# Local attention after a convolution block on one core: score tiles of 96 near keys, P turned in 32x32 blocks, values after the fourth unit

## What is computed

```python
perceived = conv3x3_depthwise(x, w_perc) + b_perc           # 128 -> 384 channels
hid = gelu(perceived @ w_up1 + b_up1)                       # 256 channels
h = x + hid @ w_up2 + b_up2
q, k, v = split(h @ w_qkv + b_qkv)
scores = stack([(q * shift(k, dy, dx)).sum(-1) for dy, dx in _POS]) / sqrt(128)   # 9 neighbours
out = h + sum_i softmax(scores)[i] * shift(v, dy_i, dx_i)
```

## Time and profile before

| | |
|---|---|
| median of 3 runs | 483.28 us (482.9 to 489.4) |
| profiled execution | 483.21 us, span of its instructions 481.4 us |
| PE busy | 443.8 us (92%), 2964 matmuls |
| DVE busy | 367.3 us (76%) |
| ACT busy | 230.4 us (48%) |
| POOL busy | 197.2 us (41%) |
| convolution matmuls (line 359) | 1728 of 256 columns, 285 to 327 ns in the record |
| scores (line 401) | 256 instructions of 192 columns, 326 ns |
| masks (line 397) | 64 of 384 columns, 329 ns |
| transposes (line 417) | 128 of 128 columns, 273 ns |
| values (line 431) | 320 of 32 to 192 columns, 305 ns |
| exponential (line 590) | 128 of 197 columns, 423 ns |
| GpSimd normalisation (line 919) | 31 of 768 elements, 1468 ns |

### The profile page before, as it was taken

The page is one execution under the profiler, slowest core; times in us unless marked ns, Lnnn a source line. Parts: engine busy times, 40 slices in busy tenths (PEclk is TensorE's granted clock), DMA queues, the critical chain, the costliest instruction groups (busy, mean ns, idle before and its releaser), DMA issues.

```text
span 481.4 us, 8443 instructions
## 1 busy us (share of the span) xinstructions
PE 443.8 (92%) x2964; PEld 388.9 (81%) x2964; DVE 367.3 (76%) x728; ACT 230.4 (48%) x491; POOL 197.2 (41%) x154
## 2 busy tenths in 40 slices
PE   1448899999999999999999999999999999999994
PEld 1437789797979899797979899797979899797863
DVE  5998768878695968878695968778695968765644
ACT  2443264554627454553627454553627354552633
POOL 3555636354451525354451525354452525320201
PEclk9966999999999999999999999999999999999999
DMA  8101020403103040403103040403013020301011
GB/s 283 70 0 60 0 103 0 146 2 100 47 21 126 2 146 0 145 0 105 40 17 128 0 145 0 145 0 113 32 26 119 0 87 0 89 9 38 0 46 44
DMA packets 11509, 29.31 MB, mean 61 GB/s; under 512 B 2400, under 2 KB 3168, under 8 KB 11488
## 3 DMA queue, kind: packets, MB, share of 16 engines
q1 hardware_dynamic: 10784, 29.03, 17.8%
q10 hardware_dynamic: 704, 0.02, 0.1%
HBM read 20.65 MB, written 8.39 MB: 60 GB/s over the span
## 4 chain that ended last, share of the span: by engine, by line
PE 81%; issue 4%; ACT 2%; DVE 1%; POOLq 0%; POOL 0%; ACTq 0%; DVEq 0%
PE m_ps L359 38%; PE work L372 11%; PE work L431 9%; PE s_ps L401 8%; PE work L378 5%; PE work L383 5%; PE work L417 3%; PE s_ps L397 2%; ACT hid L545 0%; ACT thi L529 0%; ACT p_sb L590 0%; DVE y L738 0%; POOLq L84 0%; POOL p_sb L919 0%; ACT L590 0%
## 5 line engine op out<-in xcount | busy, mean ns | idle before, releaser
L359 PE MATMUL m_ps<-thi,whi 128*128 128x256 f32 x576 | 188.6, 327 | 15.0 <-POOL wlo L928 7.1
L359 PE MATMUL m_ps<-tlo,whi 128*128 128x256 f32 x576 | 164.1, 285 | 0.0
L359 PE MATMUL m_ps<-thi,wlo 128*128 128x256 f32 x576 | 164.1, 285 | 0.0
L359 PEld LDWEIGHTS m_ps<-thi,whi 128*128 128x128 f32 x576 | 111.2, 193 | 23.3 <-issue 14.9
L919 POOL TENSOR_TENSOR p_sb<-p_sb,rsum 128x768 f32<-128x768 f32 x31 | 45.5, 1468 | 176.3 <-DVE rsum L780 176.3
L359 PEld LDWEIGHTS m_ps<-tlo,whi 128*128 128x128 f32 x576 | 111.6, 194 | 7.2 <-issue 7.2
L359 PEld LDWEIGHTS m_ps<-thi,wlo 128*128 128x128 f32 x576 | 111.2, 193 | 0.0
L912 POOL TENSOR_TENSOR tlo<-t,thi 128x1088 fp32r<-128x1088 f32 (+1 forms) x32 | 64.2, 2027 | 44.4 <-ACT thi L529 44.4
L590 ACT ACTIVATE p_sb<-s_ps,negmax 128x197 f32<-128x197 f32 x124 | 51.4, 423 | 37.6 <-DVE negmax L773 37.6
L607 ACT ACTIVATE q_sb<-work,bq_s 128x512 f32<-128x512 f32 x32 | 22.0, 689 | 85.2 <-PE work L378 85.1
L372 PE MATMUL work<-hid,w2T 128*128 128x512 f32 x120 | 54.1, 593 | 1.5 <-ACT hid L545 1.5
(11 more groups left out here) (110 smaller groups left out, 663.9 us busy)
## 6 DMA issues: line engine op xcount, KB each, us to landing
xp<-x_planes SPq DMA_DIRECT2D x16, 680.0 KB, 5.2
xr<-x_rows SPq DMA_DIRECT2D x16, 512.0 KB, 4.0
out<-o_sb SPq DMA_DIRECT2D x32, 256.0 KB, 4.1
w1T<-w SPq DMA_DIRECT2D x1, 384.0 KB, 3.3
mask_bf<-masks SPq DMA_DIRECT2D x1, 192.0 KB, 3.9
w2T<-w SPq DMA_DIRECT2D x1, 128.0 KB, 4.9
wqk_in<-w_qk SPq DMA_DIRECT2D x1, 128.0 KB, 4.8
ident<-identity SPq DMA_DIRECT2D x1, 64.0 KB, 4.8
```

The lines of the kernel that those rows point to most:

```text
L359: last = pe.matmul(m_ps[:, b, col:col + S], a[:, j, dy, half * P:(half + 1) * P], c[:, par, T_PLACE[j], dy * WIN:dy * WIN + S], start=(s = ...
```

## The change

**Scores.** A tile's query row now meets only its own three key rows: 96 key columns (`NEAR`) instead of 192. For each of the four image rows of a tile there is one product of 32 queries and 96 keys whose result lies in partitions 32 x row onwards, so it uses a strip of 32 columns of the array. Four tiles share one bank at a step of 128 columns; `scores(n, g)` is one mask product of 4 x 96 columns and 16 such products, and both groups stand after unit 6. In `p_sb` column block dk of a row of queries holds the key row dk - 1 away. The maximum is one reduction for four tiles, the exponential has 101 columns, the normalisation 384 elements.

**Turning P.** The transposes on TensorE, their copies and `edges` are gone. `turn_p(n, g)` on VectorE turns four tiles' P in 32x32 blocks, 128 partitions x 384, into `ptc`. Since each block must go to the partitions of its key row, `place_p(n)` on ScalarE copies twelve sets of blocks (4 rows of queries x 3 key rows, 32 partitions x 8 tiles x 32, two of them 7 tiles) from `ptc` to `pt`.

**Order.** `values(n, 0)` and `values(n, 1)` stand together after unit 3 and wait for all twelve copies. On VectorE `combine(n, 1)` goes ahead of the first turn and of the second reciprocal, the second turn goes between `combine_y(n, 1)` and `finish_y(n, 1)`, and from body 2 on `combine(n, 0)` goes ahead of `add_h(n, 0)`. The fp32 identity and its load are gone.

```diff
-KEYS = WINDOW + NZ
-STEP = 256
+NEAR = 3 * W
+KEYS = NEAR + NZ
+STEP = P
...
+        ptc = sb("ptc", [P, T, NEAR])
...
+        def s_bank(g):
+
+            return s_ps[:, g, :].rearrange("p (t k) -> p t k", k=STEP)
...
+            def scores(n, g):
+                if from_image(n, 2):
+
+                    pe.wait_ge(p_done, n * 8 + (4 * g - 12))
+                s = s_bank(g)[:, :, 0:NEAR]
+                pe.matmul(s, ident_bf[:, :], mask_bf[:, g:g + 4, :], start=True, stop=False, skip_group_check=True)
+                for u in range(4):
+                    for row in range(TR):
+                        q = ((4 * g + u) * TR + row) * W
+                        last = pe.matmul(s[row * W:(row + 1) * W, u, :], q_sb[:, q:q + W], h_around[:, q:q + NEAR],
+                                         start=False, stop=(u == 3 and row == TR - 1), skip_group_check=True)
                 last.then_inc(s_ready, 1)
...
             def values(n, g):
 
 
                 pe.wait_ge(v_done, n * 4 - 4)
-                pe.wait_ge(pt_done, n * 2 + (g - 3))
-                pe.wait_ge(edges_done, n * 4 + (2 * g - 6))
+                pe.wait_ge(z_done, n * 4 - 4)
+                pe.wait_ge(pt_done, n * PLACED - PLACED)
...
                 units(0)
-                if store:
-                    transpose_p(n - 1, 1)
-                units(1)
+                units(1, 2, 3)
                 if store:
                     values(n, 0)
-                units(2)
-                if store:
                     values(n, 1)
-                units(3)
...
                     project_v(n, 3)
-                    scores(n, 2)
-                units(8)
-                if attn:
-                    scores(n, 3)
-                units(9, 10, 11)
-                if attn:
-                    transpose_p(n, 0)
+                units(8, 9, 10, 11)
...
+            def place_p(n):
+
+                if isinstance(n, int) and n == 1:
+                    act.wait_ge(zeroed, 3)
+                act.wait_ge(ptc_done, n * 2)
+                if from_image(n, 2):
+                    act.wait_ge(o_ready, n * 2 - 2)
+                for row in range(TR):
+                    for dk in range(3):
+                        shift, near = divmod(row + dk - 1, TR)
+                        first, end = max(0, -shift), min(T, T - shift)
+                        col = (near + 2 - dk) * W
+                        nc.scalar.copy(pt[near * W:(near + 1) * W, first + shift:end + shift, col:col + W],
+                                       ptc[row * W:(row + 1) * W, first:end, dk * W:(dk + 1) * W]).then_inc(pt_done, 1)
...
                 if attn:
-                    take_pt(n, 0)
-                if is_last(n):
-                    take_pt(n, 1)
+                    place_p(n)
...
+            def row_max(n, g):
+
+                s = s_bank(g)
+                dve.wait_ge(s_ready, n * 2 + (g - 1))
+                for j in (2 * g, 2 * g + 1):
+                    z = v_bank(n, j)[:, 0:2 * VT].rearrange("p (t c) -> p t c", c=VT)[:, :, C:VT]
+                    dve.wait_ge(v_ready, n * 4 + (j - 3))
+                    nc.vector.tensor_tensor(s[:, 2 * j - 4 * g:2 * j - 4 * g + 2, NEAR:KEYS],
+                                            z.to_broadcast([P, 2, NZ]), z_base[:, 2 * j:2 * j + 2, :],
+                                            ALU.add).then_inc(z_done, 1)
+                dve.wait_ge(z_done, n * 4 + (2 * g - 2))
+                nc.vector.tensor_reduce(negmax[:, 4 * g:4 * g + 4], s[:, :, 0:KEYS], AX.X, ALU.max,
                                         negate=True).then_inc(rmax_done, 1)
...
+            def turn_p(n, g):
 
                 if is_last(n) and g == 1:
                     dve.wait_ge(pn_last_done, 1)
                 else:
                     dve.wait_ge(pn_done, n * 2 + (g - 1))
...
+                if from_image(n, 2):
+                    dve.wait_ge(pt_done, n * PLACED - PLACED)
+                tiles = slice(4 * g, 4 * g + 4)
+                nc.vector.transpose(ptc[:, tiles, :], p_sb[:, tiles, 0:NEAR]).then_inc(ptc_done, 1)
...
                 if more:
                     transform_ab(n + 1, 1 - par)
+                if from_image(n, 2) and conv:
+                    combine(n, 0)
                 if store:
                     add_h(n, 0)
...
-                if from_image(n, 2):
-                    if conv:
-                        combine(n, 0)
-                    if attn:
-                        sum_h(n, par)
+                if from_image(n, 2) and attn:
+                    sum_h(n, par)
...
-                if attn:
-                    sums(n, 1)
-                    edges(n, 0)
                 if conv:
                     combine(n, 1)
+                if attn:
+                    turn_p(n, 0)
+                    sums(n, 1)
+                if conv:
                     combine_y(n, 1)
+                if attn:
+                    turn_p(n, 1)
                 if conv:
                     finish_y(n, 1)
-                if attn:
-                    edges(n, 1)
```

More of the change, by code:

```diff
@@ L54, in window_masks @@
 def window_masks(dtype):
-    m = np.full((P, 4, WINDOW), NEG, dtype)
-    for kind in range(4):
+    m = np.full((P, T // 2 + 1, NEAR), NEG, dtype)
+    for kind in range(T // 2 + 1):
         for qy in range(TR):
             for qx in range(W):
-                for ky in range(-1, TR + 1):
-                    if abs(ky - qy) > 1 or (kind == 0 and ky < 0) or (kind == 3 and ky >= TR):
+                for dk in range(3):
+                    if (kind == 0 and qy + dk == 0) or (kind == T // 2 and qy + dk == TR + 1):
                         continue
                     for kx in range(max(0, qx - 1), min(W, qx + 2)):
-                        m[qy * W + place(qx), kind, (ky + 1) * W + place(kx)] = 0.0
+                        m[qy * W + place(qx), kind, dk * W + place(kx)] = 0.0
     return m
@@ L211, in build @@
         rsum_done = sem("rsum_done")
-        edges_done = sem("edges_done")
+        ptc_done = sem("ptc_done")
+        pt_done = sem("pt_done")
         pn_last_done = sem("pn_last_done")
@@ L222, in build @@
         N_W = 8
+        PLACED = TR * 3
         def steady(eng, body, last=None):
@@ L385, in project_v @@
                 last.then_inc(v_ready, 1)
-            def scores(n, j):
-                if is_last(n) and j >= 2:
-                    if j == 3:
-                        pe.wait_ge(z_done, n * 4 - 2)
-                elif j >= 2 or from_image(n, 2):
-                    pe.wait_ge(p_done, n * 8 + (2 * j - 10))
-                s = s_bank(n, j).rearrange("p (a b) -> p a b", a=2)
-                kinds = 0 if j == 0 else 2 if j == T // 2 - 1 else 1
-                pe.matmul(s[:, :, 0:WINDOW], ident_bf[:, :], mask_bf[:, kinds:kinds + 2, :], start=True, stop=False,
-                          skip_group_check=True)
-                for u in range(2):
-                    i = 2 * j + u
-                    last = pe.matmul(s[:, u, 0:WINDOW], q_sb[:, i * P:(i + 1) * P],
-                                     h_around[:, i * P:i * P + WINDOW], start=False, stop=(u == 1),
-                                     skip_group_check=True)
-                last.then_inc(s_ready, 1)
@@ L406, in transpose_p @@
-            def transpose_p(n, g):
-                if is_last(n) and g == 1:
-                    pe.wait_ge(pn_last_done, 1)
-                else:
-                    pe.wait_ge(pn_done, n * 2 + (g - 1))
-                if is_last(n):
-                    pe.wait_ge(z_done, n * 4 - 3 if g == 0 else n * 4)
-                else:
-                    pe.wait_ge(z_done, n * 4 + (0 if g == 0 else -2))
-                for u in range(4):
-                    last = pe.transpose(work[:, 1 + g, u * P:(u + 1) * P], p_sb[:, 4 * g + u, W:W + P], ident[:, :])
-                last.then_inc(pt_ready, 1)
+            def scores(n, g):
[8 more added lines that the diff above has]
+                                         start=False, stop=(u == 3 and row == TR - 1), skip_group_check=True)
+                last.then_inc(s_ready, 1)
@@ L787, in edges @@
                     dve.wait_ge(pn_done, n * 2 + (g - 1))
-                first, end = 4 * g, 4 * g + 4
-                a = max(first, 1)
-                nc.vector.transpose(pt[P - W:P, a - 1:end - 1, P + W:WINDOW],
-                                    p_sb[0:W, a:end, 0:W]).then_inc(edges_done, 1)
-                e = min(end, T - 1)
-                nc.vector.transpose(pt[0:W, first + 1:e + 1, 0:W],
-                                    p_sb[P - W:P, first:e, P + W:WINDOW]).then_inc(edges_done, 1)
+                if from_image(n, 2):
+                    dve.wait_ge(pt_done, n * PLACED - PLACED)
+                tiles = slice(4 * g, 4 * g + 4)
+                nc.vector.transpose(ptc[:, tiles, :], p_sb[:, tiles, 0:NEAR]).then_inc(ptc_done, 1)
             def add_h(n, g):
@@ L918, in normalise @@
                 pool.wait_ge(rsum_done, n * 2 + (g - 1))
```

(5 more changed lines are left out.)

69 lines of the change are left out of this document (19 added, 50 removed).

## The result

The changed kernel takes 567.49 us (median of 4 runs, 566.5 to 571.52) against 483.61 us for the kernel before (4 runs), a ratio of 1.172 with a 95% interval of 1.161 to 1.183: slower by 84 us. I had forecast 548 us, range 515 to 580. The profiled execution has a span of 565.6 us; that of before has 481.4.

What follows compares the result with a forecast made beforehand. TensorE was taken to bound the kernel at 27.0 us an image. Standstill 50, clock 10, last body 3.5, end 2.4, less 1.2 at the start, make 65 us on 483.2: 548 us, range 515 to 580.

Steps and rivals of the forecast that it cites:

- P late: Ahead of the values: the second turn stands behind combine_y, then twelve copies follow; P ready at +7.95, TensorE at +4.25.
- the standstill behind unit 3: TensorE ahead of the first value matmul, bodies 2 to 15: stands still for 3.7 us waiting for ScalarE's copies.
- the chain behind the copies: Gelu, m13, combine, add_h, transform and add_h(1) queue behind the copies; up(1) ends at +15.2, an image takes 30.6 us.
- the fallen clock: TensorE's granted clock falls after the standstill in most images, adding 0.7 us an image.
- E + 4.15: On VectorE: end of the second turn, counted from E, the moment unit 0 of the next image begins.
- the copy: ScalarE's copies of P to pt: 0.31 us each, twelve take 3.8 us; bounds 2.3 and 4.8 us.
- S: The new score stage on TensorE, masks and small products: 3.5 us an image, ends 1.8 and 5.7.
- Strips fully side by side: Rival, score stage: all four strips overlap, S = 1.8, 27 us less, 521 us; chance 15%.
- Strips in a row: Rival, score stage: products follow one another, S = 5.7, 35 us more, 583 us; chance 15%.
- the clock holds: Rival, TensorE: the clock does not fall, 10 us less, 538 us; chance 20%.
- combine_y escapes GpSimd: Rival, VectorE: the copies start 2.05 us earlier, 29 us less, 519 us; chance 8%.
- P is in time: Rival, values: copies end by +4.25, TensorE alone sets the time, 474 us, or 446 us with side-by-side strips; chance 7%.

Runs made afterwards that it cites:

- Half of the copies: Changed kernel with only six of the twelve sets of blocks copied to pt, part of P left out: 519.6 us, ratio to before 1.070.
- the early turns: Changed kernel with, on VectorE, the second reciprocal ahead of combine(n, 1) and both turns directly behind it, ahead of combine_y: 510.83 us, ratio to before 1.051.
- the split copies: The early turns plus add_h ahead of combine(n, 0), with VectorE copying four sets and ScalarE the other eight: 471.83 us, ratio to before 0.976.
- the filler: Changed kernel with 36 convolution-sized matmuls, results unread, put between unit 3 and the values: 549.84 us, ratio to before 1.133.
- The run with the other order: Changed kernel with the loops of the twelve copies swapped, key row outside and query row inside: 568.25 us, ratio to before 1.168.
- the run with four products in one strip: Changed kernel with the score loops over tile and row swapped, so four products in a row use the same 32-column strip: 596.33 us, ratio to before 1.229.
- the two versions in which P is in time: The split copies, 471.83 us; and the same with VectorE taking five sets, ScalarE seven, and add_h(1) ahead of the transform, 459.92 us.

## Why the prediction was right, and where its terms were off

**Direction and mechanism: right.** P late, the standstill behind unit 3, the chain behind the copies, the fallen clock: each was seen where it was put. Half of the copies (-48 us) and the early turns (-57 us) show that the lateness of P is the cause, the split copies on top of these take the whole loss away, and the filler shows the clock's own share. That 567 us lay inside the range is in part luck, as the sum below says: an error in the strips and errors in four other terms had opposite signs.

**When P comes.** The second turn was forecast to end at E + 4.15 and ended at 4.2; `combine` began at E - 1.8 (forecast -1.9). combine_y took 238.33 - 234.62 = 3.7 us (forecast 3.4). The term that was mis-sized is the copy: 12 x 0.31 = 3.8 us was forecast, 5.04 measured, 0.42 apart where each lasts 0.38 to 0.40. The step that failed is the choice of the row: a 128-column copy followed after 0.19 us by an instruction that reads PSUM. The row of three 256-column products, 0.40 apart, was nearer in size, and I had made it the upper bound. The run with the other order says that it is the copy's own cost. That is 1.3 us a body.

**The chain behind the copies.** From the end of the copies to the end of up I forecast 7.25 us at full clock; the filler run has 245.2 - 237.4 = 7.8. Half a microsecond, which I put down to hand-offs, was left out.

**The clock.** Forecast 0.7 us a body, measured (567.5 - 549.8) / 14 = 1.3. The fall was forecast, its size was not. The low stretch did not begin with the standstill but near its end (0.94 in 240 to 244, then 0.50), so nearly all of it fell on work: the value matmuls and up take 5.07 + 3.43 and 5.92 + 3.69 us in turn, against 3.10 + 3.43 at full clock, so 2.0 and 3.1 us are lost, 2.5 on average, where I had 2. In the filler run the same work, with its waits for `add_h`, takes 245.20 - 237.47 = 7.73 us, so the waits take up 1.2 of the 2.5. My 1.3 for them did not follow from my own times, which give 0.6 + 0.35 = 0.95. And the row from which I took the fall shows less than I read in it: in the kernel before no matmul ran from 16 to 20 us either, so 2.01 us to 27.21 was not the only idle time ahead of it.

**The strips.** S was forecast at 3.5 us (ends 1.8 and 5.7) and is 228.82 - 226.70 = 2.1, as in the rival "fully side by side", whose measure was 1.8. The argument that two halves of one product share a strip and so allow only neighbours to overlap was wrong: all four strips work at once, each with a new instruction every 83 ns, so 32 of them take 0.80 us. This took 1.4 us a body from the time. A change between whole array and strips costs little: mask to products is 226.95 - 226.70 = 0.25 us instead of 201.91 - 201.75 = 0.16. The Trainium skill, "TensorEngine Tiling (Array Packing)", Key Properties, says that a change of tiling mode drains the engine; by the trace a change costs about a tenth of a microsecond here.

**The sum.** A body came out at 32.4 us where 31.3 was forecast: copies +1.3, hand-offs +0.5, clock +0.6, strips -1.4. (The 11.9 us for the rest of TensorE's work are 11.8 by my own terms.) From up in body 15 to the end it is 565.6 - 506.5 = 59.1 us against 481.4 - 435.05 = 46.4, 12.7 more where 6 was forecast. The two sets of copies there take 5.04 us each and not 3.8, and the value groups too ran at the low clock (5.72 and 5.00 us), which the forecast had left out. Startup was 0.9 us shorter (up of body 1 at 55.26 instead of 56.16; 1.2 forecast). Had the strips behaved as forecast, S = 3.5, the same kernel would have taken, as an estimate, 567 + 16 x 1.4 = 590 us (587 if 29 of 34 us show, as in the run with four products in one strip), outside the range; that run, whose S is 4.2, took 596. So the strips' error covered those of the copies, the hand-offs, the clock and the end.

**The rivals.** *Strips fully side by side* was right in its mechanism; its 521 us did not come, because the other terms were short. *Strips in a row* and *the clock holds* fell. *combine_y escapes GpSimd* fell in the changed kernel (3.7 us) and came true in the split version (1.34). *P is in time* did not come in the changed kernel, but its figures do: it gave 446 to 474 us, and the two versions in which P is in time measure 471.8 and 459.9.

## What to carry to other kernels

A change that makes the bounding engine's work cheaper can lose several times the gain if it moves the result which that engine waits for behind work of other queues; follow the last input through every queue that it crosses, and look first at two things that cost nothing to change, what stands ahead of the producer in its queue and which engines share the copying. A standstill of TensorE has a second price in the clock of the work behind it, here 1.3 us for each one of 4.9. For a copy's cost take the row of the same size, and count the distance between starts, not the duration.

## What the hardware showed beyond what I expected

- Column strips: fp32 instructions of 96 columns on four strips in turn start in fours, 7 ns apart, every 83 ns: 32 in 0.80 us. With four products (eight instructions) in a row on one strip, 32 take 1.85 us.
- The clock fell in 13 of 13 bodies behind waits of 4.9 us, in 11 behind 2.3 us, in 6 and in 3 behind 1.9 us, and in none behind 0.2 to 0.4 us (split copies) or 0.6 to 0.7 us (filler); where it fell, the low clock came near the end of the wait, so that the work behind it paid.
- ScalarE's copies of 32 partitions x 256 elements start 0.42 us apart, as much as 256 columns on 128 partitions (0.40 apart): a quarter of the partitions costs no less. VectorE did the same copy in 0.75 and 0.78 us beside GpSimd and in 0.29 us when GpSimd had stopped.
- VectorE's `combine_y`, four instructions of 128 x 256: 3.7 us beside GpSimd, 1.34 us behind it.
